# A graph convolution on one core: the input transform of the edge stage as four 64 by 64 products on the quarters of the array

## Chip, cores and metric

The kernel runs on one core of one Trainium2 chip. The metric is the time of one execution on the device in microseconds. Before the change it is 939.04 us, the median of 3 runs (lowest 938.84, highest 939.92).

## What is computed

There are 50000 nodes with 160 features (64 scalars and 32 vectors of 3 components) and 50000 edges, sorted by destination. Cut to what matters:

```python
h  = silu(edge_scalars @ (Wfc1 / sqrt(16)))        # edge_scalars: (E, 16)
w0, w1, w2, w3 = split(h @ (Wfc2 / sqrt(64)))      # 64, 64, 32, 32 columns
e0 = (x0 @ Wl1_0 * a * inv8)[edge_src]             # 64 scalars of the source node
e1 = (einsum('num,uv->nvm', x1, Wl1_1) * a * inv32)[edge_src]   # 32 x 3
mid0 = w0 * e0 * sh0
mid1 = w3 * einsum('eum,em->eu', e1, sh1) / sqrt(3)
mid2 = w1[:, :, None] * e0[:, :, None] * sh1[:, None, :]
mid3 = w2[:, :, None] * e1 * sh0[:, :, None]
n0..n3 = segment mean of mid0..mid3 over edge_dst
conv = [n0|n1] @ Wl2_s, (n2|n3) @ Wl2_v            # and alpha = [n0|n1] @ Wa
x = layernorm(x + sc + alpha * conv)               # sc = x @ Wsc
```

Everything is float32.

## The kernel before, in words

**Two stages.** The edge stage makes a message row for each edge and stores it to device memory. The node stage then reads, for each group of 512 nodes, the windows of message rows that belong to it, sums them by a product with a one-hot matrix (L787), adds the self term and normalises. The change lies in the edge stage alone.

**The edge stage** works in steps of 4 tiles of 128 edges (QUAD); there are NS = 98 of them, and some steps are in flight at once. Tile t = 0 or 1 and pair k = 0 or 1 number the four tiles. Every engine runs the same hand-written order: `edge_steps` calls the engine's `step(d)` for d = 0, 1, ..., and between two steps of VectorE (DVE) it puts small pieces of preparation for the node stage (`between`). Engines are tied to each other by semaphores only.

**TensorE (PE)**, in `step(d)`: `first_layer(d)` (L669) is the first layer of the edge network; `turn(d, k)` transposes the gathered node rows (L675 for the scalars, L677 for the vectors, one for each t); `combine(d - 3, k)` multiplies the products with the second weights `wy` (L726 and L728) into the bank pair `y_ps[k]`; and last comes `weigh(d - 1)`: e1 (L690), e0 (L695), and the second layer of the edge network (L708). In `weigh` the e1 product of a tile t takes all 128 rows of the array: the rows are four blocks of 32 channels (the dot product with sh1, and three components), and the stationary matrix `wt[:, W_E1:W_E1 + P]` holds Wl1_1 four times on its diagonal and zeros elsewhere. The e0 products and those of L708 have 64 rows, t = 0 on the upper and t = 1 on the lower half of the array. One float32 `matmul` of the program is two weight loads and two MATMUL records in the profile.

**PSUM.** e_ps (banks 2 and 3, one for each t) shares its banks with y_ps[0]; so `weigh` waits for `msg_ready[t]`, the message that DVE makes from y_ps[0], and for `e_out[t]`, ScalarE's copy of the e of the step before.

**ScalarE (ACT)** copies h, the transposed rows (L822, L824), z (L832, from y_ps) and e (L847) out of PSUM. **DVE** multiplies w and e into mid (L969), writes a label (L977), makes z and msg of each tile (L987, L993), and prepares the operands of a later step (L944, L953, L959). **GpSimd (POOL)** issues four gathers of node rows in each step (L586) and waits for `t_ready` four steps back. **SyncE** stores the messages and loads edge features.

**Weights** are packed by the host in `pack_weights`; they come in two loads, columns up to W_YA first, the rest by L390. DVE scales the second part into `wy` once, at the start (L1180 to L1194), and `combine` of the first step waits for all 8 of these.

Of the kernel before, what the change touches and what calls it, by code (L numbers as in the profile page):

```python
# [22 lines left out]
P = 128  # L23
F32 = mybir.dt.float32
I32 = mybir.dt.int32
ALU = mybir.AluOpType
# [44 lines left out]
HALF = 64  # L71
# [16 lines left out]
W_Y1 = W_YA + MUL1 + 1 + MUL0  # L88
W_SA = W_Y1 + VEC + 1 + MUL0
W_SB = W_SA + P  # L90
WC = W_SB + P
LAST = D - P


def gnn_kernel(nc, turned, spread, x_g, src_t, dst_t, dst_rows, sh_t, ea_t, weights, out):
# [22 lines left out]
    with ExitStack() as ctx:  # L118
# [537 lines left out]
        def _(pe):  # L656
# [24 lines left out]
            def weigh(q):  # L681
                b = q % 2

                pe.wait_ge(t_out, 2 * q + 2)
                for t in range(2):
                    if q >= 2:
                        pe.wait_ge(msg_ready[t], 2 * (q - 2) + 1)
                    if q >= 1:
                        pe.wait_ge(e_out[t], q)
                    nc.tensor.matmul(e_ps[:, t, 2 * P:4 * P], wt[:, W_E1:W_E1 + P],  # L690
                                     t_sb[:, b, 1 + t].rearrange("p k e -> p (k e)"),
                                     start=True, stop=True)
                for t in range(2):
                    half = slice(t * MUL0, (t + 1) * MUL0)
                    last = nc.tensor.matmul(e_ps[:, t, 0:2 * P], wt[half, W_E0:W_E0 + P],  # L695
                                            t_sb[half, b, 0].rearrange("p k e -> p (k e)"),
                                            start=True, stop=True)
                last.then_inc(e_ready, 1)

                pe.wait_ge(h_out, 2 * q + 2)  # L700
                if q >= 1:
                    for t in range(2):
                        pe.wait_ge(mid_ready[t], q)
                for c in range(2):
                    w = W_W + c * P
                    for t in range(2):
                        half = slice(t * FC_H, (t + 1) * FC_H)
                        last = nc.tensor.matmul(w_ps[:, t, 2 * c * P:2 * (c + 1) * P],  # L708
                                                wt[half, w:w + P],
                                                h_sb[half, b].rearrange("p k e -> p (k e)"),  # L710
                                                start=True, stop=True)
                last.then_inc(w_ready, 1)

            def combine(q, k):
                p, y = 2 * q + k, y_ps[k]
                if p == 1:
                    pe.wait_ge(heads_out, 2)
                for t in range(2):
                    if p == 0:
                        pe.wait_ge(wy_ready, 8)  # L720
                    pe.wait_ge(mid_ready[t], q + 1)
                    if k == 0:
                        pe.wait_ge(e_out[t], min(q + 2, NS))
                    if q >= 1:
                        pe.wait_ge(msg_ready[t], p - 1)
                    nc.tensor.matmul(y[:, t, 0:W_Y1 - W_YA], mid[:, q % 2, t, 0, k, :],  # L726
                                     wy[:, 0:W_Y1 - W_YA], start=True, stop=True)
                    nc.tensor.matmul(y[:, t, W_Y1 - W_YA:YW], mid[:, q % 2, t, 1, k, :],  # L728
                                     wy[:, W_Y1 - W_YA:W_SA - W_YA],
                                     start=True, stop=True).then_inc(y_ready[t], 1)  # L730

            def step(d):
# [33 lines left out]
            def step(i, b):  # L766
# [8 lines left out]
                if group_alive(i, b, 1):  # L775
                    b1 = (b - 1) % 2

                    if RING * i + b == 1:
                        for t in range(2):
                            pe.wait_ge(msg_ready[t], NQ)  # L780
                    pe.wait_ge(hot_ready, groups(i, b, 1))
                    if group_has(i, b, 3):
                        pe.wait_ge(agg_ready, groups(i, b, 3))
                    for k in range(2):
                        for c in range(WC_ROWS):
                            for h in range(2):
                                last = nc.tensor.matmul(  # L787
                                    agg_ps[b1][:, 2 * h + k, 0:SW], hot[side(h), b1, k, c, :],
                                    win[side(h), (b - 1) % RING, k, c, 0:SW],
                                    start=c == 0, stop=c == WC_ROWS - 1)  # L790
                    last.then_inc(agg_done, 1)

                    pe.wait_ge(xt_out, groups(i, b, 1))
                    if group_has(i, b, 2):
                        pe.wait_ge(pre_ready, groups(i, b, 2))
                    for k in range(GROUP):
                        nc.tensor.matmul(sca_ps[:, k, :], xt[:, b1, k, :],  # L797
                                         wy[:, W_SA - W_YA:W_SB - W_YA], start=True, stop=True)
                    last = nc.tensor.matmul(scb_ps.rearrange("p k w -> p (k w)"),
                                            xt[:, b1, GROUP, :],  # L800
                                            wy[:, W_SB - W_YA:WC - W_YA], start=True, stop=True)
                    last.then_inc(sc_ready, 1)


# [120 lines left out]
        def _(dve):  # L925
# [207 lines left out]
            def between(d):  # L1133
# [41 lines left out]
                if d == FLAG + 6:  # L1175
# [3 lines left out]
            dve.wait_ge(more_weights_in, 16)  # L1179
            nc.vector.tensor_scalar(wy[:, 0:W_Y1 - W_YA], wt[:, W_YA:W_Y1], inv_fc * inv8 * inv96,  # L1180
                                    None, ALU.mult).then_inc(wy_ready, 1)
            nc.vector.tensor_scalar(wy[0:MUL1, W_Y1 - W_YA:W_SA - W_YA], wt[0:MUL1, W_Y1:W_SA],
                                    inv_fc * inv32 * inv96 * 3 ** -0.5, None,
                                    ALU.mult).then_inc(wy_ready, 1)
            for m in range(3):
                part = slice((m + 1) * MUL1, (m + 2) * MUL1)
                nc.vector.tensor_scalar(wy[part, W_Y1 - W_YA:W_SA - W_YA], wt[part, W_Y1:W_SA],
                                        inv_fc * inv32 * inv96, None,
                                        ALU.mult).then_inc(wy_ready, 1)
            nc.vector.tensor_scalar(wy[0:MUL0, W_SA - W_YA:W_SB - W_YA], wt[0:MUL0, W_SA:W_SB],  # L1190
                                    inv8, None, ALU.mult).then_inc(wy_ready, 1)
            nc.vector.tensor_scalar(wy[MUL0:P, W_SA - W_YA:W_SB - W_YA], wt[MUL0:P, W_SA:W_SB],
                                    inv32, None, ALU.mult).then_inc(wy_ready, 1)
            nc.vector.tensor_scalar(wy[:, W_SB - W_YA:WC - W_YA], wt[:, W_SB:WC], inv32,  # L1194
                                    None, ALU.mult).then_inc(wy_ready, 1)
            dve.wait_ge(dsts_in, 16)
            nc.vector.tensor_scalar(dsts_i[:], dsts_i[:], CYCLE - 1, None, ALU.bitwise_and
# [166 lines left out]
def pack_weights(np, Wfc1, Wfc2, Wsc0, Wsc1, Wl1_0, Wl1_1, Wl2_s, Wl2_v, Wa):  # L1364
# [8 lines left out]
    for s in range(2):  # L1373
# [2 lines left out]
        rows = slice(s * FC_H, (s + 1) * FC_H)  # L1376
        w[rows, W_W:W_W + P] = Wfc2[:, 0:P]
        col = W_W + P
        w[rows, col:col + MUL1] = Wfc2[:, P + MUL1:]
        for m in range(3):  # L1380
            w[rows, col + (m + 1) * MUL1:col + (m + 2) * MUL1] = Wfc2[:, P:P + MUL1]
        for c in range(2):
            w[half, W_E0 + c * MUL0:W_E0 + (c + 1) * MUL0] = Wl1_0
    w[MUL0:P, W_YA:W_YA + MUL1] = Wl2_v[:MUL0]
# [6 lines left out]
    w[0:MUL1, W_E1:W_E1 + MUL1] = Wl1_1  # L1391
    w[0:MUL1, W_Y1 + VEC] = Wa[MUL0:, 0]
    w[0:MUL1, W_Y1 + VEC + 1:W_SA] = Wl2_s[MUL0:]
    w[0:MUL0, W_SA:W_SA + MUL0] = Wsc0
    for n in range(2):
        part = slice(MUL0 + n * MUL1, MUL0 + (n + 1) * MUL1)
# [67 lines left out]
```

## Time and profile before

| what | us |
|---|---|
| median of 3 runs (lowest, highest) | 939.04 (938.84, 939.92) |
| the profiled execution, its own time | 942.17 |
| its span in the profile | 940.4 |
| PE busy | 903.4 |
| DVE busy | 810.2 |
| POOL busy | 712.5 |
| ACT busy | 631.8 |
| granted TensorE clock, mean over the span | 0.993 of full speed |

The engines' busy times are sums over both stages, and the two stages have different limits. The edge stage ends at about 548 us. PE is the engine of the MATMUL records and PEld that of the weight loads, which usually run beside the MATMULs. The ends of MATMUL records are modelled (a record of 128x256 is shown with 376 to 480 ns while the next one starts about 215 ns after it), so for PE the starts, and the chain of waits that is built on them, are what is read. "<-" names what ended an idle time.

### The profile page before, as it was taken

How to read it: one execution, taken by the hardware profiler on the slowest of the kernel's cores; microseconds unless marked ns; L12 is line 12 of the kernel's file. 1: busy time of each engine (PE TensorE's matmuls, PEld its weight loads, DVE VectorE, ACT ScalarE, POOL GpSimd, SP SyncE). 2: the span in 40 equal slices, each digit the busy share in tenths (PEclk: the TensorE clock that was granted, in tenths of full speed). 3: DMA queues.
4: the chain of work that ended last, by engine and by line, in shares of the span. 5: the costliest groups of instructions: out<-in, count | busy, mean ns of one | idle time of the engine just before them, and what ended most of it. 6: DMA issues, size and time to landing. Idle time of an engine off the chain costs nothing.

```text
span 940.4 us, 27168 instructions
## 1 busy us (share of the span) xinstructions
PE 903.4 (96%) x7944; PEld 799.0 (85%) x7944; DVE 810.2 (86%) x2793; ACT 631.8 (67%) x1961; POOL 712.5 (76%) x804
## 2 busy tenths in 40 slices
PE   2999999999999999999999989999999999999995
PEld 2788888888888888888888879998988889988994
DVE  3798899999989999888888977888888888888887
ACT  1555555555555555555555537898988888888887
POOL 6777777777777777767767317998888889888894
PEclk9999999999999999999999999999999999999998
DMA  6465554454465555456544217999999999999993
GB/s 176 118 177 153 160 141 129 131 139 130 134 120 163 157 166 139 130 157 178 143 132 127 82 75 215 313 297 308 302 292 298 294 290 304 302 311 301 306 293 142
DMA packets 87518, 186.34 MB, mean 198 GB/s; under 512 B 17646, under 2 KB 48138, under 8 KB 87371
## 3 DMA queue, kind: packets, MB, share of 16 engines
q1 hardware_dynamic: 48411, 87.64, 28.9%
q10 hardware_dynamic: 20016, 61.15, 19.6%
q0 software_dynamic: 18944, 35.81, 17.2%
q8 instruction: 66, 1.08, 0.5%
q14 instruction: 81, 0.66, 0.2%
HBM read 119.58 MB, written 64.95 MB: 196 GB/s over the span
## 4 chain that ended last, share of the span: by engine, by line
PE 64%; POOL 20%; issue 12%; DVE 2%; DMA 1%; POOLq 0%; ACT 0%; DVEq 0%; ACTq 0%
PE ps L728 12%; POOL res L639 9%; PE ps L690 9%; PE ps L708 9%; PE ps L726 8%; PE ps L695 6%; POOL xa L627 6%; PE ps L677 5%; PE ps L787 4%; PE ps L675 4%; POOL xa L623 3%; PE ps L797 2%; PE ps L669 2%; DMA gat<-spread,srcs 1%; PE ps L773 1%
## 5 line engine op out<-in xcount | busy, mean ns | idle before, releaser
L586 POOL DMA_INDIRECT gat<-turned,srcs x196 | 189.0, 964 | 74.5 <-issue 67.3
L586 POOL DMA_INDIRECT gat<-spread,srcs x196 | 189.1, 965 | 61.8 <-issue 56.0
L847 ACT ACTIVATE e_sb<-ps 128x512 f32<-128x512 f32 x196 | 106.4, 595 | 131.0 <-PE ps L695 131.0
L787 PE MATMUL ps<-win,hot 60*128 60x162 f32 x2352 | 190.5, 308 | 0.7 <-DVE hot L1310 0.7
L728 PE MATMUL ps<-wy,mid 128*128 128x161 f32 x784 | 182.3, 314 | 0.0
L787 PEld LDWEIGHTS ps<-win,hot 60*128 60x128 f32 x2352 | 166.4, 187 | 17.1 <-issue 16.5
L993 DVE SCALAR_TENSOR_TENSOR msg<-ps,sha,z 128x161 f32<-128x161 f32 x392 | 151.0, 385 | 13.9
L639 POOL TENSOR_TENSOR res<-agg,pre 128x640 f32<-128x640 f32 x98 | 151.9, 1550 | 11.4 <-ACT agg L892 11.4
L726 PE MATMUL ps<-wy,mid 128*128 128x97 f32 x784 | 141.4, 262 | 0.2 <-DVE mid L969 0.2
L969 DVE TENSOR_TENSOR mid<-ps,e_sb 128x512 f32<-128x512 f32 x196 | 133.1, 679 | 2.1 <-PE ps L708 2.1
L870 ACT ACTIVATE fin<-res,shift,rstd 128x160 f32<-128x160 f32 x292 | 132.0, 537 | 1.4 <-DVE shift L1259 1.3
L892 ACT ACTIVATE agg<-ps,coef 128x160 f32<-128x160 f32 x392 | 122.4, 407 | 8.4 <-DVE coef L1350 8.3
L726 PEld LDWEIGHTS ps<-wy,mid 128*128 128x128 f32 x784 | 123.2, 190 | 1.3 <-issue 0.7
L832 ACT ACTIVATE z<-ps 128x65 f32<-128x65 f32 x392 | 89.7, 229 | 46.0 <-PE ps L728 46.0
L728 PEld LDWEIGHTS ps<-wy,mid 128*128 128x128 f32 x784 | 119.0, 192 | 0.0
L797 PE MATMUL ps<-wy,xt 128*128 128x128 f32 x784 | 113.5, 288 | 0.2 <-DVE pre L1337 0.2
L987 DVE TENSOR_TENSOR z<-ps,sha 128x96 f32<-128x96 f32 x392 | 97.8, 250 | 15.7 <-ACT z L832 15.0
L797 PEld LDWEIGHTS ps<-wy,xt 128*128 128x128 f32 x784 | 94.8, 191 | 17.5 <-issue 17.5
L690 PE MATMUL ps<-t_sb,wt 128*128 128x256 f32 x392 | 103.0, 385 | 3.1 <-issue 3.1
L822 ACT ACTIVATE h_sb<-ps 128x128 f32<-128x128 f32 x196 | 54.3, 277 | 73.5 <-PE ps L677 62.4
L627 POOL TENSOR_TENSOR xa<-xin 128x512 f32<-128x512 f32 x98 | 102.5, 1046 | 0.0
L708 PE MATMUL ps<-h_sb,wt 64*128 64x256 f32 x784 | 101.1, 376 | 0.6 <-DVE mid L969 0.6
(105 smaller groups left out, 1611.9 us busy)
## 6 DMA issues: line engine op xcount, KB each, us to landing
win<-rows SPq DMA_DIRECT2D x392, 114.6 KB, 3.6
rows<-msg SPq DMA_DIRECT2D x98, 326.0 KB
out<-fin ACTq DMA_DIRECT2D x47, 640.0 KB, 5.3
xin<-x_g ACTq DMA_DIRECT2D x92, 322.0 KB, 4.5
gat<-turned,srcs POOLq DMA_INDIRECT x196
gat<-spread,srcs POOLq DMA_INDIRECT x196
eas<-ea_t SPq DMA_DIRECT2D x7, 384.0 KB, 5.3
xin<-x_g SPq DMA_DIRECT2D x6, 322.0 KB, 4.0
```

What stands on the lines that cost most here:

```text
L586: pool.indirect_dma_start(out=gat[:, slot, first:first + of.shape[1]], out_offset=None, in_=of, in_offset=bass.IndirectOffsetOnAxis(ap=src ...
L627: nc.gpsimd.tensor_tensor(xa[:, b0, 0:GROUP, :], xin[:, n, :, 1:1 + P], xin[:, n, :, 0:1].broadcast_to([P, GROUP, P]), ALU.mult).then_inc( ...
L639: nc.gpsimd.tensor_tensor(res[:, slot], agg[:, b3], pre[:, b3], ALU.add).then_inc(res_ready, 1)
L690: nc.tensor.matmul(e_ps[:, t, 2 * P:4 * P], wt[:, W_E1:W_E1 + P], t_sb[:, b, 1 + t].rearrange("p k e -> p (k e)"), start=True, stop=True)
L708: last = nc.tensor.matmul(w_ps[:, t, 2 * c * P:2 * (c + 1) * P], wt[half, w:w + P], h_sb[half, b].rearrange("p k e -> p (k e)"), start=Tru ...
L726: nc.tensor.matmul(y[:, t, 0:W_Y1 - W_YA], mid[:, q % 2, t, 0, k, :], wy[:, 0:W_Y1 - W_YA], start=True, stop=True)
L728: nc.tensor.matmul(y[:, t, W_Y1 - W_YA:YW], mid[:, q % 2, t, 1, k, :], wy[:, W_Y1 - W_YA:W_SA - W_YA], start=True, stop=True).then_inc(y_r ...
L787: last = nc.tensor.matmul(agg_ps[b1][:, 2 * h + k, 0:SW], hot[side(h), b1, k, c, :], win[side(h), (b - 1) % RING, k, c, 0:SW], start=c == ...
L797: nc.tensor.matmul(sca_ps[:, k, :], xt[:, b1, k, :], wy[:, W_SA - W_YA:W_SB - W_YA], start=True, stop=True)
L870: last = nc.scalar.activation(fin[:, past, k, :], res[:, past, k, :], ACT.Identity, bias=shift[:, past, k:k + 1], scale=rstd[:, past, k:k ...
L969: nc.vector.tensor_tensor(mid[:, q % 2, t].rearrange("p c k e -> p (c k e)"), w_ps[:, t], e_sb[:, t], ALU.mult).then_inc(mid_ready[t], 1)
L993: nc.vector.scalar_tensor_tensor(out=msg[:, q % 2 * QUAD + n, 0:1 + D], in0=y[:, t, Y_A:Y_C], scalar=sha[:, ring, n, 0:1], in1=z[:, k, t, ...
```

## The change

The two e1 products of 128 rows and 128 columns become four products of 64 rows and 64 columns: for each t, the upper 64 rows with the upper 64 columns of the stationary matrix, and the lower with the lower (the off-diagonal quarters hold zeros only). The result of t = 0 goes to the partitions of its own half; that of t = 1 to the other half, so that each of the four has a quarter of the array of its own. The waits for both t now stand ahead of all four. Because e1 of t = 1 now lies with its halves exchanged, the columns of Wfc2 for the odd tile are packed in exchanged order, and `combine` uses a second copy of 161 columns of `wy` for t = 1, with its row halves exchanged. That copy makes the second load of weights 161 columns longer, and DVE scales it with four more instructions at the start.

```diff
-WC = W_SB + P
+W_Y1B = W_SB + P
+WC = W_Y1B + VEC + 1 + MUL0
...
                     if q >= 1:
                         pe.wait_ge(e_out[t], q)
-                    nc.tensor.matmul(e_ps[:, t, 2 * P:4 * P], wt[:, W_E1:W_E1 + P],
-                                     t_sb[:, b, 1 + t].rearrange("p k e -> p (k e)"),
-                                     start=True, stop=True)
+                for n in range(2):
+                    for t in range(2):
+
+                        half = slice(n * HALF, (n + 1) * HALF)
+                        made = slice((n + t) % 2 * HALF, ((n + t) % 2 + 1) * HALF)
+                        nc.tensor.matmul(e_ps[made, t, 2 * P:4 * P],
+                                         wt[half, W_E1 + half.start:W_E1 + half.stop],
+                                         t_sb[half, b, 1 + t].rearrange("p k e -> p (k e)"),
+                                         start=True, stop=True)
...
                     if p == 0:
-                        pe.wait_ge(wy_ready, 8)
+                        pe.wait_ge(wy_ready, 12)
...
+                    of = (W_Y1, W_Y1B)[t] - W_YA
                     nc.tensor.matmul(y[:, t, W_Y1 - W_YA:YW], mid[:, q % 2, t, 1, k, :],
-                                     wy[:, W_Y1 - W_YA:W_SA - W_YA],
+                                     wy[:, of:of + VEC + 1 + MUL0],
                                      start=True, stop=True).then_inc(y_ready[t], 1)
...
-            nc.vector.tensor_scalar(wy[0:MUL1, W_Y1 - W_YA:W_SA - W_YA], wt[0:MUL1, W_Y1:W_SA],
-                                    inv_fc * inv32 * inv96 * 3 ** -0.5, None,
-                                    ALU.mult).then_inc(wy_ready, 1)
-            for m in range(3):
-                part = slice((m + 1) * MUL1, (m + 2) * MUL1)
-                nc.vector.tensor_scalar(wy[part, W_Y1 - W_YA:W_SA - W_YA], wt[part, W_Y1:W_SA],
-                                        inv_fc * inv32 * inv96, None,
-                                        ALU.mult).then_inc(wy_ready, 1)
+            for t, of, width in ((0, W_Y1, W_SA - W_Y1), (1, W_Y1B, WC - W_Y1B)):
+                for m in range(4):
+
+                    part = slice((m + 2 * t) % 4 * MUL1, ((m + 2 * t) % 4 + 1) * MUL1)
+                    nc.vector.tensor_scalar(wy[part, of - W_YA:of - W_YA + width],
+                                            wt[part, of:of + width],
+                                            inv_fc * inv32 * inv96 * (1 if m else 3 ** -0.5),
+                                            None, ALU.mult).then_inc(wy_ready, 1)
...
-        w[rows, col:col + MUL1] = Wfc2[:, P + MUL1:]
-        for m in range(3):
-            w[rows, col + (m + 1) * MUL1:col + (m + 2) * MUL1] = Wfc2[:, P:P + MUL1]
+        for m in range(4):
+
+            made = col + (m + 2 * s) % 4 * MUL1
+            part = Wfc2[:, P:P + MUL1] if m else Wfc2[:, P + MUL1:]
+            w[rows, made:made + MUL1] = part
...
+    for half in range(2):
+        other = slice((1 - half) * HALF, (2 - half) * HALF)
+        w[half * HALF:(half + 1) * HALF, W_Y1B:WC] = w[other, W_Y1:W_SA]
```

## Rows read from the trace of the kernel before

**Rows 1.** Busy time of each engine in the edge stage and the node stage.

```profile
core 0: us, PE busy (x) PEld busy (x) DVE busy (x) ACT busy (x) POOL busy (x), PEclk, DMA share, GB/s
25.00:548.00 523.00, 519.25 (x4035) 454.19 (x4034) 471.17 (x1370) 296.14 (x958) 371.00 (x394) 1.00 0.51 141
548.00:940.00 392.00, 375.63 (x3875) 338.47 (x3873) 331.19 (x1402) 330.44 (x991) 324.12 (x384) 0.98 0.87 277
```

**Rows 2.** Chain of waits, one edge step: start us, us, what.

```profile
299.93 0.86 PE ps L690 x4
300.79 0.63 PE ps L695 x4
301.43 0.86 PE ps L708 x8
302.29 0.22 PE ps L669 x4
302.51 0.26 PE ps L675
...
303.98 0.11 PE ps L675
...
305.31 0.86 PE ps L690 x4
```

**Rows 3.** Waits in 25 to 548 us: us in total, times, longest us.

```profile
DVE z L987 <- ACT z L832: 14.8, 51, 0.7
DVE sha L944 <- DMA gat<-spread,srcs: 9.1, 7, 2.1
...
PEld ps L690 <- DVE msg L993: 2.5, 10, 0.3
...
DVE mid L969 <- PE ps L708: 1.5, 2, 0.8
```

**Rows 4.** Timeline: start us, us, engine line op [idle before].

```profile
303.83 0.26 DVE L987 TENSOR_TENSOR z<-ps,sha 128x96 f32<-128x96 f32 x1
...
304.72 0.38 DVE L993 SCALAR_TENSOR_TENSOR msg<-ps,sha,z 128x161 f32<-128x161 f32 x1
...
305.01 0.76 PEld L690 LDWEIGHTS ps<-t_sb,wt 128*128 128x128 f32 x4
...
305.14 1.03 PE L690 MATMUL ps<-t_sb,wt 128*128 128x256 f32 x4
...
306.10 0.30 PEld L695 LDWEIGHTS ps<-t_sb,wt 64*128 64x128 f32 x4 [0.33 <-issue]
306.10 0.70 PE L695 MATMUL ps<-t_sb,wt 64*128 64x256 f32 x4
306.30 0.95 POOL L586 DMA_INDIRECT gat<-turned,srcs  x1 [0.30 <-issue]
...
306.64 1.03 PE L708 MATMUL ps<-h_sb,wt 64*128 64x256 f32 x8
...
307.55 0.94 POOL L586 DMA_INDIRECT gat<-spread,srcs  x1 [0.30 <-issue]
```

**Rows 5.** Timeline of PE, 301.26 to 301.29 us.

```profile
301.26 0.38 PE L708 MATMUL ps<-h_sb,wt 64*128 64x256 f32 x2
```

**Rows 6.** Waits in 440 to 520 us.

```profile
DVE z L987 <- ACT z L832: 4.4, 15, 0.3
```

**Rows 7.** Timeline of the start of the kernel.

```profile
13.24 0.88 DVE L1187 TENSOR_SCALAR wy<-wt 32x161 f32<-32x161 f32 x3
...
18.08 0.17 DVE L944 TENSOR_TENSOR sha<-shs,gat 128x16 f32<-128x16 f32 x1 [2.33 <-DMA gat<-spread,srcs]
```

More of the change, by code:

```diff
@@ L800, in step @@
                                             xt[:, b1, GROUP, :],
-                                            wy[:, W_SB - W_YA:WC - W_YA], start=True, stop=True)
+                                            wy[:, W_SB - W_YA:W_Y1B - W_YA], start=True, stop=True)
                     last.then_inc(sc_ready, 1)
@@ L1193, in _ @@
                                     inv32, None, ALU.mult).then_inc(wy_ready, 1)
-            nc.vector.tensor_scalar(wy[:, W_SB - W_YA:WC - W_YA], wt[:, W_SB:WC], inv32,
+            nc.vector.tensor_scalar(wy[:, W_SB - W_YA:W_Y1B - W_YA], wt[:, W_SB:W_Y1B], inv32,
                                     None, ALU.mult).then_inc(wy_ready, 1)
```

## The prediction, made before the changed kernel was run

> **What bounds the kernel now.** I read the stages first, then the chain of waits, then who waits for whom. In the edge stage, which the change touches, PE is busy for 519 of 523 us, DVE for 471 and POOL for 371 [rows 1]; the clock is granted in full, its 2.4 GHz level. The chain of waits confirms PE: a whole step of it is PE work only, and the same piece comes back after 305.31 - 299.93 = 5.38 us [rows 2], one step. With 98 steps this is 527 us. PE is therefore the bound, but not by far, and the second reading is how much room the others have. In the steps where DVE has nothing else to do, its only idle time that another engine makes is 4.4 us in 15 steps, 0.29 us a step, waiting for ACT's copy of z [rows 6]. DVE could thus run a step in 5.38 - 0.29 = 5.09 us. Over the whole stage, with the small preparations between the steps, it waits 14.8 us for that copy and 1.5 us for L708 [rows 3]: 16.3 us is what DVE can give back before it is the bound itself. (The 9.1 us for gathers is a wait for memory, which a faster PE does not shorten of itself.) POOL issues a gather every 307.55 - 306.30 = 1.25 us when nothing holds it [rows 4], so four take 5.00 us; it is the third limit.
>
> **What the part that changes costs now.** From the first e1 record to the first of L708 PE takes 306.64 - 305.14 = 1.50 us [rows 4]. Its terms: four e1 records at 0.215 us, 0.86 us in all [rows 2]; then the first e0 record starts 306.10 - 305.14 = 0.96 us after the first e1 record [rows 4], 0.10 later than the e1 work ends; and from there to L708 it is 0.54 us [rows 4], where two rounds of 0.215 would be 0.43, so 0.11 more. Those 0.10 and 0.11 us are what it costs to go from 128-row products to 64-row ones: the weight load of L695 starts with its MATMUL at 306.10, after 0.33 us in which nothing was loaded [rows 4], while L690's load came 0.13 us ahead. I read it as a pause to empty the array (0.10) and a weight load of 128 columns that nothing covers (0.11). The way back shows the same sort of cost, 0.26 us for L675 after L669 against 0.11 within 128-row work [rows 2]. Products on the two row halves do run together: two L708 records start in the same instant [rows 5], and 8 of them take as long as 4 of L690, 0.86 us [rows 2].
>
> **The change, part by part.**
> - *e1.* Four matmuls give eight records of 64 rows and 64 columns, each with 256 moving columns. The trace has no product narrower than 128 columns of weights, so this is bounded from the nearest rows. Lower bound: all four quarters work at once, two rounds, 0.43 us. Upper bound: only the row halves overlap, as in L708, four rounds, 0.86 us, the same as now. I take 0.43: the four have quarters of their own and write to different banks wherever they write the same partitions, which is just the condition under which the two halves of L708 overlap fully; what I carry over without a row is that it holds for columns as for rows.
> - *Going into e1.* The pause that stood ahead of e0 now stands ahead of e1: 0.10, and an uncovered load, of 64 columns: between 0 and the 0.11 of L695; I take half of the latter, 0.05, as it has half the columns. Sum 0.15.
> - *From e1 to e0.* e0 stays at 64 rows by 128 columns. If a change of columns alone needs no pause this costs 0; if it is like a change of rows, 0.10 + 0.11 = 0.21. I take 0.21, since the only change of shape that the trace has, in either direction, costs about that. The Trainium skill, TensorEngine Tiling (Array Packing), section Key Properties, speaks against this change here: going from one tiling mode to another drains the engine, so both borders would pay; the trace agrees for rows, and for columns no row shows it. By that rule it is 0.21, without it 0.
> - *New sum.* 0.15 + 0.43 + 0.21 + 0.43 (e0) = 1.22 us against 1.50: 0.28 us saved in a step. A PE step becomes 5.10 us. The ends: 1.01 with no second pause (0.49 saved), 1.65 with four rounds and both pauses (0.15 lost).
> - *The waits moved ahead.* All four products now stand behind `msg_ready[1]` and `e_out[1]`. The message it speaks of ends at 304.72 + 0.38 = 305.10, and e1 starts at 305.14 [rows 4]; so now it costs nothing, but there is no room left. Behind it on PE stand e0 and L708, and ACT's copy of e and DVE's mid wait for them. Already now L690 is held by that message 10 times, 2.5 us [rows 3]. It will be the place where PE waits once DVE is the bound. The chain from turn through ACT's copies and DVE's z (303.83) to the message has fixed lengths, and moves with PE; it contains the shortened part too and sets no period above 5.10.
> - *combine and the weights.* L728 reads another copy of the same size: same count and shape, nothing. Host packing: nothing.
> - *Start.* Four more scalings at 0.88/3 = 0.29 us are 1.2 us on DVE. They are hidden by the 2.33 us that DVE waits for gathers at 18.08 [rows 7]; without that cover they would cost 1.2 us. The second load of weights grows by 161 x 4 x 128 bytes = 82 KB, 0.6 us at the 141 GB/s of the stage [rows 1]; it delays gathers by between 0 and 0.6 us, and I take 0.
> - *Node stage.* Nothing.
>
> **The sum.** PE alone would give 98 x 0.28 = 27 us. But DVE's step is 5.09, and over the stage it can give 16.3 us before it has no wait left. PE at 5.10 and DVE at 5.09 are a tie, and two engines at a tie do not meet without small waits; I leave 2 us for that: 14 us. The profiled execution took 942.17 us with a span of 940.4, so its like after the change is 928.2 us. The median of the runs is 3.1 us below the profiled execution; the forecast for it is 939.04 - 14 = **925 us**. What 0.2% is (1.9 us) is about what a measurement of this kernel can tell from no change.
>
> **The rivals.**
> - *Quarters in turn (932 us).* A matmul here is two records, and the records of one tile must follow each other. If a row half takes its records in order, as A1 A2 B1 B2 for the two quarters, B1 can only start beside A2: three rounds, 0.65 us, not two. Then the saving is 0.28 - 0.215 = 0.07 us, 98 x 0.07 = 7 us: 932 us; without the second pause it is 0.28 and DVE's cap again, 925. For it: each half then has two matmuls in a row. Against it: the halves of L708 stand in the program in the same way, and start together [rows 5]. The Trainium skill, TensorE: Matmul & The Clock Gate, section Part 3 (What overlaps and what doesn't), has MATMULs start strictly in program order. By that rule this rival is the outcome; the pairs of L708 start earlier than such an order of whole matmuls would let them, so the trace bears it out only in part.
> - *The columns don't overlap (953 us, slower).* The change then doesn't do what it says: the two quarters of a row half share the way of the moving data and go one after the other. e1 keeps its four rounds, 0.86 us, and the step pays the entry of 0.15 a second time: 98 x 0.15 = 14 us more, 953 us. It decides as soon as e1 in quarters takes more than 0.71 us with both pauses. For it: no row shows two products on the same rows at once. Against it: the two read different data (tile t = 0 and t = 1) and write different partitions and banks, so they share nothing else that the code shows.
> - *No pause between e1 and e0, but four rounds (933 to 939 us).* 0.15 + 0.86 + 0.43 = 1.44, 0.06 saved, 6 us or less with the message's wait.
> - *DVE as a soft bound (916 us).* If earlier gathers also shorten some of the 9.1 us of waits for memory [rows 3], up to 23 us come back.
>
> **How the numbers follow.** Forecast, with what ends at DVE's cap whatever the pauses are: 0.52. Quarters in turn with both pauses: 0.20. Columns in sequence, slower: 0.20. Few rounds gained or nothing: 0.08. The likeliest case alone spans 918 to 930. The range takes in the soft bound and the quarters in turn, and leaves out the slower case: 916 to 941. Faster by over 0.2%: 0.52 + 0.20 + half of 0.08, less a little for waits I don't see, 0.75. Same 0.05, slower 0.20.
>
> **What would show it.** In the profile after: eight e1 records a step, four of them starting together, and the next four 0.215 us later; the first L708 record 1.22 us after the end of combine; the chain of waits no longer PE alone, with DVE's L987, L993 and L969 in it; the wait of L690's successor for DVE's msg grown from 2.5 us to 10 or more, and DVE's wait for ACT's z, 14.8 us now, near zero. A step of 5.2 us on average. It is wrong if the e1 records start one or two at a time, or if the chain is still all PE with a period of 5.3 or more.

## The result, and the profile after

On the same chip, 14 runs of each, the changed kernel takes 934.33 us (929.9 to 937.92) and the kernel before 940.23 (936.61 to 942.6): ratio 0.9933, 95% interval 0.9917 to 0.9949. That is faster by 5.9 us, on the side forecast and inside the range of 916 to 941, but 8.1 us short of the 14 us of the forecast.

| what | before | after |
|---|---|---|
| median | 940.23 | 934.33 |
| profiled execution, its span | 942.17, 940.4 | 932.28, 930.5 |
| PE busy | 903.4 | 880.9 |
| DVE busy | 810.2 | 812.1 |
| first e1 record, last e1 record | 20.93, 548.34 | 20.47, 542.04 |
| a quiet step (DVE without preparations) | 5.38 | 5.22 |
| mean step, first e1 to last e1 | 5.44 | 5.38 |

The edge stage ends 6.3 us earlier; what the two profiled executions differ by beyond that lies in the node stage, which the change doesn't touch, and the medians don't show it.

The windows of the two stages after (us; busy time and count for PE, PEld, DVE, ACT, POOL; granted clock as a share of full speed; DMA share; GB/s), against [rows 1]:

```profile
25.00:548.00 523.00, 504.57 (x4460) 420.65 (x4459) 477.16 (x1387) 299.34 (x968) 372.46 (x394) 1.00 0.52 142
548.00:930.00 382.00, 367.16 (x3830) 331.68 (x3829) 325.67 (x1385) 327.97 (x982) 324.78 (x384) 0.99 0.89 283
```

The clock is granted in full in the edge stage as before (its 2.4 GHz level), so it is no part of the difference. PE is no longer busy all the time, and DVE, at 477 us, is not yet full either: neither engine alone is the bound over the whole stage.

The chain of waits of the changed kernel in a quiet step, against [rows 2]:

```profile
430.61 0.66 PE ps L696 x8
431.27 0.63 PE ps L702 x4
431.91 0.86 PE ps L715 x8
432.77 0.22 PE ps L670 x4
...
435.49 0.30 PE ps L736 x2
435.79 0.05 issue
435.84 0.66 PE ps L696 x8
```

435.84 - 430.61 = 5.23 us a step. The chain still names only PE, with one new piece, the 0.05 us of issue ahead of e1. The changed part takes 0.05 + 0.66 + 0.63 = 1.34 us where it took 0.86 + 0.63 = 1.49, so 0.15 is saved in a step, not 0.28.

The same stretch in the timeline of the changed kernel; the first fence is PE's row alone for 435.84 to 435.87:

```profile
435.84 0.45 PE L696 MATMUL ps<-t_sb,wt 64*64 64x256 f32 x4
```
```profile
435.20 0.39 DVE L1001 SCALAR_TENSOR_TENSOR msg<-ps,sha,z 128x161 f32<-128x161 f32 x1
435.32 0.47 PE L736 MATMUL ps<-wy,mid 128*128 128x161 f32 x2
435.81 0.24 PEld L696 LDWEIGHTS ps<-t_sb,wt 64*64 64x64 f32 x8 [0.26 <-ACT t_sb L832]
435.84 0.66 PE L696 MATMUL ps<-t_sb,wt 64*64 64x256 f32 x8
436.43 0.30 PEld L702 LDWEIGHTS ps<-t_sb,wt 64*128 64x128 f32 x4 [0.38 <-issue]
436.43 0.70 PE L702 MATMUL ps<-t_sb,wt 64*128 64x256 f32 x4
436.97 1.03 PE L715 MATMUL ps<-h_sb,wt 64*128 64x256 f32 x8
```

Four e1 records start within 0.03 us: the four quarters do work at once. Two things are to be seen in the rest. The e0 load again waits until the array is free (0.38 us without a load), so the second change of shape is paid. And the message that e1 waits for ends at 435.20 + 0.39 = 435.59, but the first load comes only at 435.81. The releaser named there, ACT's t_sb, had ended by 435.48; it is one of five waits that stand ahead of e1 in PE's queue (t_out, then msg_ready and e_out of t = 0, then of t = 1), and a row can name only one.

The starts of the loads in the trace settle what e1 waits for. After the change the first load of e1 comes 0.22 us after the end of t = 1's message, in quiet steps and in steps with preparations alike. Before the change it stood 0.09 us ahead of that end in a quiet step (305.01 against 305.10, [rows 4]), because only the second e1 product waited for that message. So a loop stands behind the chain's rows of PE: message, 0.22 us, e1, and through combine, ACT's copies and DVE to the next message. The kernel waits_last_2 below, which shortens only the 0.22, shortens the step.

The waits of the stage, 25 to 548 us (total, times, longest), against [rows 3]:

```profile
PEld ps L696 <- ACT t_sb L832: 29.3, 90, 0.7
PE ps L696 <- DVE msg L1001: 12.8, 25, 2.2
DVE sha L952 <- DMA gat<-spread,srcs: 8.4, 7, 2.3
DVE z L995 <- ACT z L840: 2.5, 4, 1.4
DVE mid L977 <- PE ps L715: 2.2, 4, 0.7
```

DVE's wait for ACT's z has gone from 14.8 us to 2.5, and PE waits for DVE's message 25 times, 12.8 us, where it was 10 times, 2.5 us. The new row is the first: in 90 of the 98 steps the load engine is idle for 0.3 us ahead of e1, behind the waits of PE's own queue.

**Where the rest of the quiet step's gain went.** 0.155 us (5.38 against 5.22, unrounded) in 97 steps would be 15 us; 6.3 came, 0.5 of them ahead of the first e1. DVE's preparation for step 53 is one row in each kernel and marks the middle. The first is of the kernel before, the second of the changed one:

```profile
296.03 0.17 DVE L944 TENSOR_TENSOR sha<-shs,gat 128x16 f32<-128x16 f32 x1
```
```profile
294.51 0.16 DVE L952 TENSOR_TENSOR sha<-shs,gat 128x16 f32<-128x16 f32 x1
```

The first half gains 1.5 us, the second 548.34 - 296.03 against 542.04 - 294.51, so 252.3 against 247.5 us: 4.8. Two losses are visible in the trace. One is in steps in which DVE has preparations for the node stage. They take 5.3 to 5.6 us after the change, for instance the one between these two rows, 5.45:

```profile
324.64 0.66 PE L696 MATMUL ps<-t_sb,wt 64*64 64x256 f32 x8 [0.27 <-DVE msg L1001]
330.09 0.66 PE L696 MATMUL ps<-t_sb,wt 64*64 64x256 f32 x8 [0.27 <-DVE msg L1001]
```

The chain of waits between them is DVE's from end to end (two rows of it, one a preparation):

```profile
327.45 0.54 DVE widest L1098
328.00 0.60 DVE mid L977
```

There are 23 steps with larger pieces of preparation, and after the change they lie 4.8 us over 23 quiet ones; before it they lay only 0.2 us over. The other loss is in waits for gathers. POOL issues the gathers back to back, most of them every 1.25 us, and in the middle of the stage DVE, and PE behind it, wait for one:

```profile
264.22 0.95 POOL L587 DMA_INDIRECT gat<-spread,srcs  x1 [0.30 <-issue]
265.47 0.95 POOL L587 DMA_INDIRECT gat<-turned,srcs  x1 [0.30 <-issue]
...
277.47 0.17 DVE L952 TENSOR_TENSOR sha<-shs,gat 128x16 f32<-128x16 f32 x1 [2.26 <-DMA gat<-spread,srcs]
...
281.06 0.66 PE L696 MATMUL ps<-t_sb,wt 64*64 64x256 f32 x8 [2.18 <-DVE msg L1001]
```

Four gathers are 5.0 us a step, but POOL has other issues too, 3 us at step 14 and 5 us at step 38. The first of the four at step 38:

```profile
204.29 0.95 POOL L596 DMA_INDIRECT res<-dst_rows,at_tile_i  x1 [0.30 <-issue]
```

With these the lead of a gather over its use (from the end of a step's last issue to DVE's use) falls: after the change from 7.7 us at step 38 to 3.3 at step 41, before it from 7.9 to 3.7. At step 48 it is 5.8 us before the change and 4.5 after it. POOL's last gather for step 49 ends at 267.5 us before and at 265.2 after, 2.3 us earlier, where 49 shorter quiet steps would be 7.6.

POOL's pace alone does not make the wait, though. The last gather that DVE waits for at 277.47 is the third row here, issued until 270.17, and in front of it SyncE has issued two stores:

```profile
265.17 0.44 SPq L447 DMA_DIRECT2D rows<-pads  x1
266.24 0.40 SPq L452 DMA_DIRECT2D starts_dram<-starts  x1
...
269.23 0.94 POOL L587 DMA_INDIRECT gat<-spread,srcs  x1 [0.31 <-issue]
```

By the semaphore events of the trace that gather lands 7.1 us after its issue; 2.1 us is the median, and at step 41 a lead of 3.3 us made no wait. The second store writes one number for each tile of nodes. Some 560 packets of 4 bytes stand in the trace within 2.5 us of its issue, and in the 7 us behind them the packets of the gathers take about 1 us each on average, where the mean of the stage before is 0.2. In all 20 traces kept for this case the slowest landings of gathers after the first six steps (6 to 10 us) follow this pair of stores.

**The account, step by step.** From the first e1 to the last, 5.8 us came of the 15 that 97 quiet steps promise, so 9.2 are missing in these two executions: 4.7 in the 23 steps with preparations, 2.6 in the two steps around the wait in the middle, 1.2 in the first 17 steps, where DVE waits for gathers too, and 0.7 elsewhere.

### The profile page after: what moved, and what is told of

The parts are those of the page before. It is cut to its first block, busy times and chain, and to the rows that moved or that the text cites. A ratio compares the mean times of both kernels' runs of the same rounds, so it can differ in the third digit from the quotient of the medians.

```text
span 930.5 us, 27956 instructions
## 1 busy us (share of the span) xinstructions
PE 880.9 (95%) x8336; PEld 758.5 (82%) x8336; DVE 812.1 (87%) x2797; ACT 632.5 (68%) x1961; POOL 714.5 (77%) x804
## 4 chain that ended last, share of the span: by engine, by line
PE 46%; POOL 22%; issue 17%; DVE 11%; DMA 3%; ACT 1%; POOLq 0%; DVEq 0%; ACTq 0%
PE ps L795 7%; POOL res L640 7%; PE ps L736 7%; POOL gat L587 6%; PE ps L715 5%; POOL xa L628 5%; PE ps L733 4%; PE ps L805 4%; PE ps L696 4%; PE ps L702 4%; DVE mid L977 3%; PE ps L678 3%; POOL xa L624 3%; DVE z L995 2%; DMA gat<-spread,srcs 2%
## 5 line engine op out<-in xcount | busy, mean ns | idle before, releaser
L832 ACT ACTIVATE t_sb<-ps 128x384 f32<-128x384 f32 x196 | 95.0, 485 | 0.0
```

## The experiments

The theories: **W**, the waits in PE's queue ahead of e1 cost the missing 0.12 us a step; **D**, DVE is the bound wherever PE no longer is; **G**, the gathers' supply (POOL's issues) caps the first half; **S**, the second change of shape is what costs.

The first four kernels ran on a chip on which all kernels take about 15% longer (the kernel before 1078.52 us, 1071.73 to 1084.54, 21 runs); their traces are read here for single pieces, and three of them were taken up again on a chip like the first.

**waits_last**: the same waits, those that are fulfilled early ahead of the late one.

```diff
                 for t in range(2):
-                    if q >= 2:
-                        pe.wait_ge(msg_ready[t], 2 * (q - 2) + 1)
                     if q >= 1:
                         pe.wait_ge(e_out[t], q)
+                for t in range(2):
+                    if q >= 2:
+                        pe.wait_ge(msg_ready[t], 2 * (q - 2) + 1)
```

> The changed kernel with the waits ahead of e1 in another order: both for e_out (long met) first, both for msg_ready last. Nothing else is changed. In the changed kernel's trace e1's first weight load starts 0.32 us after the start of the last record of combine, where the end of that record's columns would be at 0.14 and a pause of 0.10, as before e0, would give 0.23. Theory 1, the waits: PE's sequencer reaches msg_ready[1] late and then has another wait behind it, so that about 0.08 us of each step are sequencing. Then the load starts at 0.22 to 0.25 us, the quiet step goes from 5.22 to 5.14 or 5.15 us, and the time falls by 3 to 8 us against the changed kernel, to a ratio of 0.985 to 0.990 against the kernel before. Theory 2, the array: the pause from 128x128 to 64x64 is simply longer, 0.18. Then nothing moves: 0.32, 5.22, ratio 0.993.

Measured: 1088.52 us, 1.0105 [1.0064, 1.0146]. The piece did move: counted from the start of combine's last record, the first e1 load comes at 0.23 instead of 0.32 us, and L716 0.10 earlier. The ratio is far from the 0.985 to 0.990 expected.

**tile_outer**: the loops exchanged, so that both quarters of t = 0 stand ahead of the waits of t = 1.

```diff
                         pe.wait_ge(e_out[t], q)
-                for n in range(2):
-                    for t in range(2):
+                    for n in range(2):
```

> The changed kernel with t as the outer loop of e1: the two quarters of t = 0 stand behind the waits for t = 0 alone, the two of t = 1 behind theirs, as in the kernel before. Theory 1 (the waits for both t ahead of all four cost time): the first weight load comes at 0.2 us after the last record of combine instead of 0.32, the quarters of t = 1 follow some 0.1 us later, and L715 starts up to 0.1 us earlier than now (1.38 to 1.48 us); ratio 0.987 to 0.993. Theory 2 (array pause): the first load stays at 0.32, ratio 0.993.

Measured: 1088.86, 1.0123 [1.0086, 1.016]; load at 0.23, second layer at 1.36. The same 0.1 us as above by another way. Neither time tells anything of W, since the changed kernel alone is 1.1% slower than before on such a chip (after_beside, below).

**before_waits_ahead**: the kernel before, with nothing changed but that all waits stand ahead of both e1 products.

```diff
                     if q >= 1:
                         pe.wait_ge(e_out[t], q)
+                for t in range(2):
                     nc.tensor.matmul(e_ps[:, t, 2 * P:4 * P], wt[:, W_E1:W_E1 + P],
```

> The kernel before with one part of the change alone: the waits for both t ahead of both e1 products, which keep their 128 rows. The prediction's step: it costs nothing now, since the message is done at 305.10 and e1 starts at 305.14. Theory 1 (waits): the weight load can't run ahead any more, e1 starts 0.05 to 0.15 us later than the end of combine, a step grows from 5.38 to 5.43 to 5.53 us, the time by 5 to 14 us (ratio 1.005 to 1.015). Theory 2: within 1 us, ratio 1.000.

Measured: 1083.78, 1.0054 [1.0024, 1.0084]. The e1 load now comes 0.33 us after the start of combine's last record, where it came beside it (0.00), and the second layer 1.93 after it instead of 1.63.

**half_rows**: e1 as two products of 64 rows and 128 columns, so that it has e0's shape. It leaves out half of the components of e1.

```diff
-                for n in range(2):
-                    for t in range(2):
...
+                for t in range(2):
+                    half = slice(t * HALF, (t + 1) * HALF)
+                    nc.tensor.matmul(e_ps[:, t, 2 * P:4 * P], wt[half, W_E1:W_E1 + P],
+                                     t_sb[half, b, 1 + t].rearrange("p k e -> p (k e)"),
+                                     start=True, stop=True)
```

> The changed kernel with e1 computed from half of its rows only: t = 0 from the upper, t = 1 from the lower 64 rows, each 64 rows by 128 columns, as e0 is. It leaves out half of the components of e1. Two rounds of 0.215 us as the quarters, but the same shape as e0 behind it, so the change of shape between e1 and e0 falls away. If that change costs what the prediction gave it (0.21 us, the changed trace shows about 0.20), L715 starts 1.28 us after the last record of combine instead of 1.48. If the narrow products themselves are the slow ones, it starts only 0.05 to 0.1 earlier. The step: PE then has 5.02 us of work, so whatever limits the step instead shows: 5.09 to 5.12 if DVE's own work is the limit, 5.02 if PE still is, 5.2 if the loop PE, ACT, DVE through the message is of fixed length whatever PE does.

One execution, 1080.72 us. Its timeline:

```profile
438.90 0.33 PEld L693 LDWEIGHTS ps<-t_sb,wt 64*128 64x128 f32 x4 [0.35 <-issue]
439.44 0.63 PE L698 MATMUL ps<-t_sb,wt 64*128 64x256 f32 x4
439.87 1.06 PE L711 MATMUL ps<-h_sb,wt 64*128 64x256 f32 x8
```

From the first e1 load to the second layer it is 0.97 us, against 436.97 - 435.81 = 1.16 in the changed kernel. Both have two rounds of e1 and two of e0; what differs is the change from 64x64 to 64x128, so that costs 0.19 us. S is right as a piece, and was in the sum (0.21).

**On a chip like the first** (the kernel before 939.89 us, 935.93 to 947.68, 13 runs) four kernels ran side by side.

**after_again**, the changed kernel once more, as the measure for the rest.

> The changed kernel as it is, beside the others of this call, since the four runs before it were on a chip where the kernel before itself takes 1078 us. If that chip is used again, a ratio above 1.00 is expected for it too (the two variants that were faster in the trace of a step gave 1.010 and 1.012 there); on a chip where the kernel before takes 940 us, 0.993 and a quiet step of 5.22 us.

934.05 us, 0.9935 [0.9906, 0.9963]: the first result again. Its steps with preparations lie 4.8 us over quiet ones, as in the first trace. Its waits for gathers lie elsewhere: the two steps in the middle are only 0.8 us over (3.7 in the first trace), the first 17 steps 7.4 (4.5), and the lead at step 48 is 5.8 us, as in the kernel before.

**waits_ahead_2**, before_waits_ahead once more.

> The kernel before with the waits for both t ahead of both e1 products and nothing else. On the other chip e1's first load came 0.33 us after the last record of combine began, instead of 0.00, and L708 0.30 us later. Theory 1: here too, 0.15 to 0.30 us a step, since the loop through the message then has the whole of e1 behind it: a step of 5.5 to 5.65 and a ratio of 1.015 to 1.03. Prediction's own step (it costs nothing): 1.000.

965.78 us, 1.0268 [1.0233, 1.0304], 26 us slower. Its timeline shows the piece:

```profile
430.38 0.39 DVE L994 SCALAR_TENSOR_TENSOR msg<-ps,sha,z 128x161 f32<-128x161 f32 x1
430.99 0.73 PEld L691 LDWEIGHTS ps<-t_sb,wt 128*128 128x128 f32 x4 [0.26 <-ACT t_sb L825]
```

The message ends at 430.77. The first e1 load, which stood 0.09 us ahead of that end in the kernel before, now starts 0.22 after it, and a step takes 5.66 us, 0.28 more. So moving the waits ahead costs as much, on its own, as the whole change was to save. In the changed kernel part of that is hidden, since the array has to run empty for the change of shape anyway.

**waits_last_2**, waits_last once more.

> As waits_last: the waits for e_out ahead of those for msg_ready. In its trace e1's first weight load came 0.09 us earlier (0.23 instead of 0.32 us) and L715 0.10 us earlier, as theory 1 said. What is open is the step: 5.22 less 0.10 is 5.12 if the loop PE, ACT, DVE through the message sets it; DVE's own work sets 5.09 as a floor. So 5.12 to 5.14 in quiet steps and a ratio of 0.985 to 0.990. If DVE is the limit of most steps already, the step stays at 5.20 to 5.22 and the ratio at 0.993.

932.02 us, 0.9913 [0.9887, 0.994]. A quiet step is 5.12 us instead of 5.23, and its chain of waits is no longer PE's. Three rows of it; the first and the last are one step apart:

```profile
429.79 0.68 DVE mid L978
431.77 0.68 DVE mid L978
434.91 0.69 DVE mid L978
```

434.91 - 429.79 = 5.12 us, with DVE's rows and its issue between them. Those 0.11 us in 97 steps would be 10 us; 2 came, and the two intervals overlap. The ratio expected was 0.985 to 0.990. In the profiled execution, at 936.3 us the slowest of its six, the time went into waits, PE's for DVE's message and DVE's for a gather:

```profile
PE ps L697 <- DVE msg L1002: 17.0, 30, 2.9
DVE sha L953 <- DMA gat<-spread,srcs: 11.3, 7, 3.0
```

The load comes 0.12 to 0.14 us after the message here, against 0.22. W is right for the quiet step and D takes over right behind it.

**label_on_act**: both reorderings (e_out first, t as the outer loop), and DVE's copy of the labels is given to ACT; SyncE's store waits for it.

```diff
+                if q >= 1:
+                    for t in range(2):
+                        pe.wait_ge(e_out[t], q)
                 for t in range(2):
                     if q >= 2:
                         pe.wait_ge(msg_ready[t], 2 * (q - 2) + 1)
-                    if q >= 1:
-                        pe.wait_ge(e_out[t], q)
...
+                    nc.scalar.activation(msg[:, half, LABEL], dsts[:, QUAD * q:QUAD * (q + 1)],
+                                         ACT.Copy).then_inc(label_ready, 1)
...
-                nc.vector.tensor_copy(msg[:, half, LABEL], dsts[:, QUAD * q:QUAD * (q + 1)]
-                                      ).then_inc(label_ready, 1)
```

> e_out waits first, t as the outer loop of e1, and the copy of labels (L985, 0.16 us a step) moved from DVE to ACT, which has over 1 us idle in a step; the store waits for it. Theory DVE (in the steps with preparations for the node stage DVE's sum of work is the limit, and in quiet steps the loop through the message): quiet steps 5.10 to 5.13, set by PE or the loop, and the steps of 5.3 to 5.5 us fall by 0.15 each; ratio 0.980 to 0.986. Rival (the preparations cost because they stand inside the loop, not because of DVE's sum): those steps fall by less than 0.05 against waits_last_2.

927.53 us (925.52 to 931.85), 0.9884 [0.9856, 0.9911]: 12.4 us under the kernel before, and faster than both kernels of this study, though short of the 0.980 to 0.986 expected. Its chain of waits:

```profile
433.66 0.59 PE ps L697 x8
434.25 0.63 PE ps L703 x4
434.88 0.86 PE ps L716 x8
...
438.76 0.59 PE ps L697 x8
```

5.10 us a step, and 0.59 + 0.63 = 1.22 us for e1 and e0 with no issue ahead of them. A step with DVE's preparations is 5.37 us instead of 5.45:

```profile
329.56 0.93 PE L697 MATMUL ps<-t_sb,wt 64*64 64x256 f32 x8
334.93 0.93 PE L697 MATMUL ps<-t_sb,wt 64*64 64x256 f32 x8
```

A smaller load on DVE shortens the steps that D names, by 0.08 us; 0.15 was expected by D and less than 0.05 by its rival, so it bears D out only in part. But DVE's preparation for step 53 stands at 295.19 us here (294.66 in after_again, 297.96 in waits_last_2): no version gets through the first half faster than the changed kernel does, though their quiet steps differ by 0.11. The lead of the gather over its use at step 48 is down to 3.1 us, and DVE's longest wait for a gather, 4.3 us, comes at step 49, behind the same two stores. That speaks for the supply, of which POOL's pace is one part and the slow landing the other.

**late_before, late_after, late_best**: G was to be tested by putting POOL's and SyncE's other issues later, past the place where the gathers run short, in the kernel before, the changed one and label_on_act.

```diff
-CONSTANTS = 14
-TABLES = 18
-STARTS = 44
-FLAG = 56
-WINDOWS = 34
+CONSTANTS = 34
+TABLES = 38
+STARTS = 64
+FLAG = 76
+WINDOWS = 44
```

> The kernel before with the preparations for the node stage 20 steps later (CONSTANTS, TABLES, STARTS, FLAG up by 20, WINDOWS by 10): POOL's own extra work of 3 and 5 us and the first loads of node rows then come when the gathers are further ahead. Theory supply (in the first half of the edge stage POOL issues gathers without a pause, one step in 5.0 us plus 8 us of extra work, and stalls of up to 8 us in landing eat the lead; so a faster PE only finds a smaller lead): here PE needs 5.38 us, the lead is ample and little changes: 0.996 to 1.000 of the kernel before. Rival (the stalls are at fixed places in the work of DVE and PE): no change at all, 1.000.

> The changed kernel with the same preparations 20 steps later. Theory supply: the operands of step 53 are prepared at 294.5 us in the changed kernel against 296.0 in the kernel before, 1.5 us for 50 shortened steps; with the lead kept up, step 53 comes 3 to 6 us earlier, and the time falls to 0.984 to 0.990 of the kernel before, that is 3 to 8 us below the changed kernel. Rival (DVE's own sum of work has taken the gain, wherever its preparations stand): within 1.5 us of the changed kernel, 0.992 to 0.995.

> label_on_act (e_out waits first, t outer, labels on ACT) with the preparations 20 steps later. It took 927.5 us with quiet steps of 5.11, but its step 53 was prepared at 295.2 us, no earlier than in the other kernels. Theory supply: step 53 comes 5 to 10 us earlier, 918 to 924 us, a ratio of 0.977 to 0.983. Rival: 0.988 as label_on_act.

> As half_rows, on whichever chip the other three run on: e1 from half of its rows, t = 0 from the upper and t = 1 from the lower 64, so that e1 and e0 have one shape (half of the components of e1 are left out). The first run gave 0.97 us from e1's first weight load to L715, 0.19 less than the quarters' 1.16: the second change of shape costs 0.19. Here the step shows what follows: PE alone would need 5.22 - 0.19 = 5.03 us, DVE's own work 5.12 (the quiet step of waits_last_2, whose chain of waits is all DVE). So 5.10 to 5.14 and a chain with DVE in it.

These and their repeats all ran on chips like that of the first four. Beside the kernel before at 1066.77 us: late_before 1067.85, 1.0013 [0.9988, 1.0038]; late_after 1081.17, 1.0112 [1.0059, 1.0164]; late_best 1078.19, 1.0105 [1.0056, 1.0155]; half_rows once more, one execution, 1072.91, on which the step of 5.10 to 5.14 us that was expected can't be read.

> As late_before, whose call went to a chip on which the kernel before takes 1067 us. On a chip where it takes 940: theory supply 0.996 to 1.000, rival 1.000.

> As late_after. On a chip where the kernel before takes 940 us: theory supply (the first half of the stage runs at POOL's pace of gathers, with its extra work and the slow landings) 0.984 to 0.990, step 53 prepared 3 to 6 us earlier than the changed kernel's 294.5; rival (DVE's own sum) 0.992 to 0.995. On the other chip, 1.01 again.

> As late_best. On a chip where the kernel before takes 940 us: theory supply 0.977 to 0.983, rival 0.988. On the other chip, 1.01 again.

> The changed kernel, to be compared with the three others on whichever chip they run. Where the kernel before takes 940 us: 0.9935. On the chip of the earlier two calls (1067 to 1078 us) it hasn't run; both its variants were 1 per cent slower than the kernel before there, so 1.005 to 1.015 if that comes with the quarters, 1.000 if it came with the variants' order of waits.

Beside the kernel before at 1065.89: late_before_2 1065.11, 1.0002 [0.9969, 1.0035]; late_after_2 1078.43, 1.0098 [1.0062, 1.0133]; late_best_2 1077.63, 1.0101 [1.0059, 1.0142]; the changed kernel itself, after_beside, 1077.04, 1.0111 [1.0073, 1.0148].

> As late_after, for a chip where the kernel before takes 940 us: theory supply 0.984 to 0.990, with the operands of step 53 prepared 3 to 6 us earlier than the changed kernel's 294.5; rival (DVE's own sum) 0.992 to 0.995. If the call goes to a chip of the other kind: 1.01, and the question stays open.

> As late_best: theory supply 0.977 to 0.983 where the kernel before takes 940 us, rival 0.988; on a chip of the other kind 1.01.

Beside 1066.07: late_after_3 1082.72, 1.0141 [1.0097, 1.0185]; late_best_3 1080.17, 1.0135 [1.0094, 1.0177].

On these chips putting the issues later changes nothing in the time (late_after_2 against after_beside), but the edge stage has another limit there (below), so what G costs is not tested by them; it rests on the traces alone. One thing they do show: the edit puts SyncE's two stores 20 steps later as well, and the slow landings go with them. In the eight traces of late_before, late_after and late_best the slowest gathers are those of steps 70 to 72 (7 to 10 us), in the others those of steps 49 to 52. So the slow landings in the middle belong to the stores and not to the place in the stage. Which of the two stores it is, no run separates. A version with e0 and the second layer in quarters too, which would save the second change of shape, wasn't tried: e0's quarters would write a bank in which the other row half of e1 is still writing, with nothing between to put them in order but that change of shape.

## Why the prediction was right in sign and too large in size

- *Four quarters at once*: right. The rivals of quarters in turn and of columns that don't overlap fell with the row of four starts. The rule by which the first of them would have come out (the Trainium skill, TensorE: Matmul & The Clock Gate, section Part 3 (What overlaps and what doesn't)) would, as I read it, have spread these starts over three rounds; four starts within 0.03 us don't bear that reading out.
- *The second change of shape*: right, 0.19 against 0.21. The Trainium skill, TensorEngine Tiling (Array Packing), section Key Properties, has the engine drained at each change of mode; the trace now agrees for columns too, by half_rows.
- *The new sum, 1.22 us*: right for the shape, as label_on_act shows (0.59 + 0.63, step 5.10), but not for the kernel as it is, where it is 1.34.
- *"The waits moved ahead: so now it costs nothing"*: wrong, and the step that failed for PE. What I read from [rows 4] was that the message ended 0.04 us ahead of e1. But that is the MATMUL; its weight load started at 305.01, 0.09 us before the message ended, so even by these rows there was no room. I put no price on the waits themselves: several waits behind the late one, and a weight load that can no longer run ahead. It is 0.12 us a step (1.34 against 1.22), and 0.28 on the kernel before (waits_ahead_2). This term alone takes the quiet step from 5.10 to 5.22. In the time it is the smaller of the two failures: 2.0 us came back when the late waits were put last, and that is not certain by itself.
- *DVE's floor of 5.09*: right, 5.12 in the chain of waits_last_2. *"Over the whole stage it can give 16.3 us"*: wrong in how it was used, and the step of the sum that failed. A sum over the stage is no store that every step can draw on. The quiet steps had 0.29 us each and the steps with preparations less than they needed, so there DVE was the bound at 5.3 to 5.6 us. Only 2 us were left for a tie. The sum took 14 us from this room; the edge stage gave 6.3, and the steps with preparations alone cost 4.7 us more than before, in after_again as well.
- *POOL as "third limit" at 5.00, and a wait for gathers that "a faster PE does not shorten"*: the second is what happened (9.1 us before, 8.4 after). In the first, POOL's 8 us of other issues were left out, and so were the two stores behind which gathers land late. The waits for gathers cost 2.6 us more than before in the middle and 1.2 in the first 17 steps; they move from one execution to the next, and no run has tested what they cost.
- *The size.* 8.1 us of the forecast 14 are missing. That 97 quiet steps at the measured 0.15 us are about 15 us, near the forecast, is luck: the step was to save 0.28, and the sum was capped by DVE's 16.3. The mean step, expected at 5.2 us, is 5.38. Waits in order give back 2.0 (934.05 to 932.02, not certain by itself), and a DVE that does less, with the loops exchanged, another 4.5 (to 927.53; the two edits weren't run apart): together 6.5 us, and 12.4 in all against the kernel before. These the runs show, the second for a kernel in which DVE does less than in the one that was forecast; the rest is waits for gathers or unexplained.
- *What would show it*: the chain was still all PE, which I had named as a mark of being wrong if its period were 5.3 or more; it is 5.23. The growth of PE's wait for the message (to 10 or more: 12.8) and the end of DVE's wait for z (near zero: 2.5) came as written.

## What to carry to other kernels

Price a wait that moves ahead of a group of products even when its semaphore has just been set: it stops the weight load that ran ahead, and each further wait behind the late one adds to it, so put the late one last. An engine's idle time is room only in the steps that have it; cut a stage into steps with and without extra work before capping a gain with it, and add up all that the supplying queue issues, not only its gathers. Look at how late gathers land as well as at when they are issued: here they come late behind two stores, one of them in single numbers. A PE product packed into quarters pays two changes of shape unless its neighbours have its shape: here about 0.1 us going in (the load at 0.23 us in waits_last, where combine's last record is done after about 0.15) and 0.19 going out.

## What the runs showed of the hardware that was not expected

**The sign depends on the chip.** In both comparisons in which the kernel before takes 940 us the change gives 0.993; where that takes 1065.89 us it gives 1.0111. Four of the chips used behave in the second way. The traces of the longer chips show no lower granted clock that would explain it (0.979 against 0.995 for 15% of time). What they do show is that about once a step PE's completions reach the other engines up to 2 us late, several at once. In half_rows on such a chip (timeline):

```profile
434.39 0.38 PE L678 MATMUL ps<-ident,gat 128*128 128x128 f32 x2
436.24 0.43 PE L729 MATMUL ps<-wy,mid 128*128 128x97 f32 x2 [1.47 <-issue]
436.50 0.95 POOL L587 DMA_INDIRECT gat<-turned,srcs  x1 [2.07 <-PE ps L678]
```

The transpose that POOL waits for ends at 434.77, and POOL goes on at 436.50. The wait table of after_beside, 25 to 600 us, has it as a sum:

```profile
POOL gat L587 <- PE ps L678: 151.0, 78, 2.8
ACT e_sb L855 <- remote: 109.6, 37, 14.1
```

Steps are 6.5 to 6.8 us there. Why the signals come late, and why it costs the changed kernel more, is open: no run was made on it.

**Products on quarters overlap in full in float32**, though each is two records, and the record rows name their weights as 64x64.
